# Routing weights spread by DMA from device memory instead of by a matmul, in a fused attention and expert kernel

## The reference, cut to what matters

```
x = x + xattn(layernorm(x), ctx)    # 16 heads of 8: causal self attention plus attention to 64 context rows
h = layernorm(x)                    # 1024 tokens
aff = sigmoid(h @ Wr + br)          # 32 experts
top_v, top_i = top_k(aff, 8);  top_w = top_v / (sum(top_v) + 1e-9)
w_full[t, e] = top_w where e is among token t's eight, else 0
shared = (silu(h @ Wg_s + bg_s) * (h @ Wu_s + bu_s)) @ Wd_s + bd_s
routed = sum over e of w_full[:, e] * ((silu(h @ Wg[e] + bg[e]) * (h @ Wu[e] + bu[e])) @ Wd[e] + bd[e])
x = x + shared + routed
```

## Time and profile before

| | |
|---|---|
| median of 3 runs | 205.09 us (204.45 to 206.31) |
| the profiled execution | 207.16 us |
| its span | 205.40 us, 3982 instructions |
| granted TensorE clock, mean | 0.981 of full speed |
| PE, DVE, ACT, POOL busy | 190.5, 160.7, 135.7, 97.9 us |
| DMA | 10.40 MB, 51 GB/s on average |

### The profile page before, as it was taken

One profiled execution on the slowest core, in us unless ns is written; L12 is line 12 of the kernel. 1 busy time (PEld: TensorE's weight loads), 2 busy tenths in 40 slices (PEclk: granted clock), 3 DMA queues, 4 the chain that ended last, 5 costly groups with the idle time before them and its releaser, 6 DMA issues.

```text
span 205.4 us, 3982 instructions
## 1 busy us (share of the span) xinstructions
PE 190.5 (93%) x1237; PEld 140.4 (68%) x1249; DVE 160.7 (78%) x375; ACT 135.7 (66%) x272; POOL 97.9 (48%) x154
## 2 busy tenths in 40 slices
PE   7969899999999999788999899699899999999993
PEld 2537667777777777666675776488688887887662
DVE  2888997788689977996594889748957879877982
ACT  3544898787898889886779453645545655555571
POOL 6899972343463757339455386665522231100020
PEclk9996999999999999999999999979999999999998
DMA  4365333233342334201201112210000000000003
GB/s 114 94 137 145 100 78 84 50 73 83 71 121 67 77 86 102 54 0 42 65 15 38 38 40 54 51 32 0 3 0 3 0 0 2 0 0 3 0 0 102
DMA packets 20434, 10.40 MB, mean 51 GB/s; under 512 B 11881, under 2 KB 18542, under 8 KB 20414
## 3 DMA queue, kind: packets, MB, share of 16 engines
q1 hardware_dynamic: 19290, 9.24, 18.2%
q0 software_dynamic: 672, 0.69, 1.5%
q10 hardware_dynamic: 452, 0.23, 0.5%
HBM read 4.51 MB, written 0.52 MB: 25 GB/s over the span
## 4 chain that ended last, share of the span: by engine, by line
PE 69%; DVE 11%; issue 8%; ACT 5%; POOL 4%; DMA 1%; DVEq 0%; POOLq 0%; ACTq 0%
PE psum L1358 10%; PE psum L1360 9%; PE psum L1359 9%; PE psum L1461 6%; PE psum L1517 5%; PE psum L1542 4%; PE psum L1554 4%; POOL hid_lo L707 3%; PE psum L1522 3%; PE psum L1564 3%; PE psum L1460 2%; PE psum L1689 2%; PE psum L1526 2%; PE psum L1503 2%; PE psum L1483 2%
## 5 line engine op out<-in xcount | busy, mean ns | idle before, releaser
L925 ACT ACTIVATE gate<-psum,bias_cols 128x512 f32<-128x512 f32 (+2 forms) x35 | 23.5, 675 | 31.5 <-PE psum L1360 31.5
L802 ACT ACTIVATE probs<-psum 128x512 f32<-128x512 f32 x64 | 36.3, 596 | 1.9 <-PE psum L1522 0.8
L707 POOL TENSOR_TENSOR hid_lo<-hid,hid_hi 128x512 fp32r<-128x512 f32 x13 | 16.7, 1287 | 32.7 <-ACT hid_hi L934 30.5
L1302 DVE SCALAR_TENSOR_TENSOR gated<-psum,bias_cols,gate 128x512 f32<-128x512 f32 x32 | 24.0, 749 | 10.5 <-ACT gate L925 7.9
L934 ACT CAST hid_hi<-hid 128x512 fp32r<-128x512 f32 (+1 forms) x33 | 20.2, 613 | 6.3 <-DVE hid L1314 4.5
L1461 PE MATMUL psum<-key_blocks,query_rows 96*128 96x512 f32 x48 | 24.1, 544 | 0.0
L1314 DVE TENSOR_TENSOR hid<-gated,psum 128x512 f32<-128x512 f32 x32 | 21.9, 683 | 2.8 <-PE psum L1689 1.1
L638 POOL TENSOR_TENSOR w_late_lo<-w_ffn,w_late_hi 128x384 fp32r<-128x384 f32 x11 | 12.3, 1116 | 20.0 <-ACT w_late_hi L814 20.0
L663 POOL TENSOR_SCALAR_AFFINE_SELECT probs<-probs 128x512 f32<-128x512 f32 x16 | 10.1, 634 | 20.7 <-ACT probs L802 20.6
L1092 DVE TENSOR_REDUCE row_max<-psum 128x4 fp32r<-128x1024 f32 x16 | 19.4, 1214 | 0.0
L1088 DVE TENSOR_REDUCE row_max<-psum 128x4 fp32r<-128x512 f32 x16 | 11.0, 689 | 8.6 <-PE psum L1461 8.5
(11 more groups left out here) (198 smaller groups left out, 515.1 us busy)
## 6 DMA issues: line engine op xcount, KB each, us to landing
query_rows<-queries SPq DMA_DIRECT2D x46, 64.0 KB, 2.0
key_rows<-keys SPq DMA_DIRECT2D x39, 32.0 KB, 1.9
w_ffn<-in_L_ffn_Wg SPq DMA_DIRECT2D x16, 64.0 KB, 2.0
w_ffn<-in_L_ffn_Wu SPq DMA_DIRECT2D x16, 64.0 KB, 2.1
w_ffn<-in_L_ffn_Wd SPq DMA_DIRECT2D x16, 64.0 KB, 2.1
ckey_rows<-ckeys POOLq DMA_DIRECT2D x12, 32.0 KB, 2.0
key_rows<-keys POOLq DMA_DIRECT2D x9, 32.0 KB, 2.0
x_sb<-in_x SPq DMA_DIRECT2D x2, 128.0 KB, 2.9
```

What stands on the lines that cost most here:

```text
L707: pool.tensor_tensor(hid_lo[:, n % 3, :], hid[:, n % 3, :], hid_hi[:, n % 3, :].bitcast(F32), ALU.subtract).then_inc(pool_lo_done, 1)
L802: act.activation(probs[:, i % 2, c, :], bank(B_ST + c % 2), ACT.Exp, scale=SCALE).then_inc(exp_done, 1)
L925: act.activation(gate[rows_of(n), n % 3, part], psum[of, B_GATE + n % 2, part], ACT.Silu, bias=bias_cols[of, BIAS_GATE + u:BIAS_GATE + u + ...
L1302: dve.scalar_tensor_tensor(out=gated[:, n % 3, :], in0=bank(B_UP + n % 2), scalar=bias_cols[:, BIAS_UP + u:BIAS_UP + u + 1], in1=gate[:, n ...
```

## The change

The spreading matmul goes, with its 0/1 matrix. ACT copies the turned weights a second time, from partitions 64 to 95 of the PSUM bank into `route_rows` (DVE now writes a third, unrounded copy of the weights into `route`, and the row of ones moves from 64 to 96). SP stores them to a tensor in device memory, once per chunk, waits for that store, and then issues one DMA per routed item: it reads the two rows of the unit's experts 64 times each into one of four slots of `wide`. The last six units' weight loads stand between these in SP's queue. DVE multiplies the gate by `wide` first, then takes (up + bias) times that.

```diff
+B_GATES = (0, 1, 4)
+B_UP, B_SIDE = 2, 5
+        route_dram = nc.dram_tensor("route_dram", (EXPERTS, TOKENS), F32, kind="Internal").ap()
 sync:
-            for u in range(SLOTS // 2, UNITS):
+            for u in range(SLOTS // 2, SLOTS + 5):
                 load_unit(sp, u)
+            for n, (u, c) in enumerate(WORK):
+                if n == 1:
+                    load_unit(sp, SLOTS + 5)
+                if LEAD // 2 <= n < LEAD // 2 + UNITS - LEAD:
+                    load_unit(sp, LEAD // 2 + n)
+                if u == SHARED:
+                    continue
+                r = routed(n)
+                cols = slice(c * CHUNK, (c + 1) * CHUNK)
+                if u == 0:
+                    sp.wait_ge(route_rows_ready, 2 * c + 2)
+                    sp.dma_start(route_dram[:, cols], route_rows[RAW:ONES, cols]).then_inc(route_stored, 16)
+                    sp.wait_ge(route_stored, 16 * (c + 1))
+                if r >= WIDE_SLOTS:
+                    sp.wait_ge(gated_done, r - WIDE_SLOTS + 1)
+                sp.dma_start(wide[:, r % WIDE_SLOTS, :],
+                             route_dram[2 * u:2 * u + 2, cols].unsqueeze(1)
+                             .to_broadcast([2, INNER, CHUNK])).then_inc(in_wide_route[r % WIDE_SLOTS], 16)
 scalar:
+                    act.copy(route_rows[RAW:ONES, tokens(b)], psum[RAW:ONES, B_MISC, 0:SEQ]).then_inc(route_rows_ready, 1)
                     act.copy(routeT[:, tokens(b)], bank(B_MISC, SEQ)).then_inc(routeT_ready, 1)
...
-                        act.activation(gate[rows_of(n), n % 3, part], psum[of, B_GATE + n % 2, part], ACT.Silu,
+                        to = gate[INNER:P, n % 3, part] if u == SHARED else gate_bank(n)
+                        act.activation(to, gate_bank(n)[of, part], ACT.Silu,
 vector:
-                    dve.wait_ge(m_up, routed(n + 1))
                     dve.wait_ge(gate_done, n + 1)
-                    dve.scalar_tensor_tensor(out=gated[:, n % 3, :], in0=bank(B_UP + n % 2), ...
+                    dve.wait_ge(in_wide_route[routed(n) % WIDE_SLOTS], 16 * (routed(n) // WIDE_SLOTS + 1))
+                    dve.tensor_tensor(gated[:, n % 3, :], gate_bank(n), wide[:, routed(n) % WIDE_SLOTS, :],
+                                      ALU.mult).then_inc(gated_done, 1)
...
+                    dve.wait_ge(m_up, routed(n + 1))
                     dve.wait_ge(gated_done, routed(n + 1))
-                    dve.tensor_tensor(hid[:, n % 3, :], gated[:, n % 3, :], bank(B_WIDE + n % 2),
+                    dve.scalar_tensor_tensor(out=hid[:, n % 3, :], in0=bank(B_UP + n % 2), ...
 gpsimd:
+            def expand(i):
+                pool.wait_ge(*keys_of(*divmod(i, GROUPS)))
+                pool.wait_ge(m_st, 4 * (i - RING) + 4)
+                for j in (0, 1):
+                    blocks, rows, mine = key_block(i, j)
+                    pool.tensor_tensor(blocks, rows, mine.to_broadcast([ROWS, SEQ]),
+                                       ALU.mult).then_inc(pool_blocks_set, 1)
             for i in range(STEPS):
+                if POOL_BLOCKS <= i + 3 < STEPS:
+                    expand(i + 3)
...
-        POOL_LO = [*range(LEAD), LAST_ITEM - 2]
+        POOL_LO = [*range(LAST_ITEM - 1)]
 tensor:
-            run_idle(8, B_CK)
+            run_idle(12, B_CK)
...
             turn_max(0)
+            run_idle(3, B_MISC)
...
-                        if n >= 2:
-                            pe.wait_ge(gated_done, routed(n - 1))
+                        if n >= 2:
+                            pe.wait_ge(hid_done, n - 1)
...
-                    if u != SHARED and n != LEAD:
-                        spread_routes(n)
```

More of the change, by code:

```diff
@@ L31 @@
 RING = 4
+POOL_BLOCKS = 5
 EXPERTS, TOP, INNER = 32, 8, 64
-SPREADS = 4
-SPREAD_UNITS = 4
+WIDE_SLOTS = 4
+RAW = 2 * EXPERTS
+ONES = 3 * EXPERTS
 PAIRS = EXPERTS // 2
@@ L191, in build @@
         in_ffn = [sem(f"in_ffn{k}") for k in range(SLOTS)]
+        route_stored = sem("route_stored")
+        in_wide_route = [sem(f"in_wide_route{k}") for k in range(WIDE_SLOTS)]
         placed_k = [[sem(f"placed_k{k}_{g}") for g in range(GROUPS)] for k in range(2)]
@@ L402, in lo_done, with gate_bank, affinity_of @@
             return hid_lo_done, VECTOR_LO.index(n) + 1
+        def gate_bank(n):
+            return bank(B_GATES[n % len(B_GATES)])
+        side = bank(B_SIDE, 6 * EXPERTS).rearrange("p (n t e) -> p n t e", n=3, t=2)
+        side_sigmoid, side_affinity, side_logits = side[:, 0, :, :], side[:, 1, :, :], side[:, 2, :, :]
+        def affinity_of(b):
+            return affinity[:, :, :] if b < 2 else side_affinity
         def routed(n):
@@ L717, in _ @@
                     split_unit(ROUND_AT[n + 1])
-            for u in range(LEAD, UNITS):
-                split_unit(u)
-            lower_half(POOL_LO[-1])
         @block.scalar
@@ L891, in left_over @@
                     if name == "router":
+                        act.wait_ge(logits_ready, b + 1)
+                        act.activation(logits[:, :, :], logits[:, :, :], ACT.Identity,
+                                       bias=tiny[:, 0:1]).then_inc(logits_guarded, 1)
                         act.wait_ge(logits_guarded, b - 1)
-                        act.activation(exp_neg[:, :, :], logits[:, :, :], ACT.Silu).then_inc(silu_ready, 1)
+                        act.activation(side_sigmoid, logits[:, :, :], ACT.Silu).then_inc(silu_ready, 1)
+                    elif name == "norm":
+                        act.wait_ge(have_rstd, len(NORM_GROUPS) + b + 1)
+                        for t in range(2):
+                            k = 2 * b + t
+                            act.activation(x2_norm[:, t, :], x1[:, k, :], ACT.Identity, scale=rstd[:, k:k + 1],
+                                           bias=neg_mean[:, k:k + 1]).then_inc(x2_normed, 1)
                     else:
```

139 lines of the change are left out of this document (57 added, 82 removed).

## The result

The changed kernel takes 301.07 us in the median of 4 runs (300.71 to 301.27), the kernel before 204.98 beside it: a ratio of 1.463, with a 95% interval from 1.456 to 1.470. Forecast were 310 us, between 197 and 335. The profiled execution took 301.27 us, its span 299.5.

What follows compares the result with a forecast made beforehand. PE bounds the late expert stage; two engines per spread would make DMA the limit. Copy at 106.3, store 1.9, 32 spreads at 5.8, weights 4.7, landing 2, tail 9.3: span 309.8, say 310 us, range 197 to 335.

Steps and rivals of the forecast that it cites:

- Two engines: Spread DMAs: source of two outer rows is cut in two, 5.8 us per item; 310 us in all, chance 0.55.
- Weights copied at 106.3: Start of the sum: the copy ends at 109.3, less the 3 us gained before.
- 185.6 + 4.7 + 2 = 192.3: Spread stage: 32 spreads at 5.8 us, last six units' weights on the same engines, last landing's fixed part.
- The tail: From gated of item 32 to the end, 9.3 us, taken from the profile of the kernel before.
- Rival A: All sixteen engines carry a spread: span 199.7, 199.4 us by the median, faster than before; chance 0.33.
- round trips at items 0 and 12: Expert stage: waits for copied weights, store and first spread make item 0 2.7 us later and lose 3 us at 12.
- key blocks on POOL: Stretch from 80 to 108: 22 operations at 0.62 us fit POOL's waits; gain 2 us, between 0 and 2.5.
- idle matmuls: Start, 10 to 20 us: they may lift the granted clock from 0.83; gain 1 us, between -1 and +1.7.
- the -2 for swapped operations: Silu bank, PSUM affinity, ACT's copies: may free PE idle time from 107.88 to 149.75; 2 us, 0 to 3.9.
- 32 spreading matmuls: Expert stage: each removed matmul saves PE 0.232 us, 7.4 us in all, the most its steady part can win.
- POOL's lower halves: Expert stage: POOL takes them from DVE, some tenths late where it also splits weights; cost 1 us, 0 to 6.
- Rival C: As sixteen engines, but stores or landings at 5 us and no idle time won back: 209 us, chance 0.04.

Runs made afterwards that it cites:

- two-DMA kernel: The changed kernel with each item's spread as two DMAs, one per expert row copied to 64 partitions, instead of one: 211.61 us, ratio 1.024 against the kernel before.
- without round trips: The kernel with two DMAs per item, but spreads read rows of input x, so nothing is stored and no spread waits for weights: 204.45 us, ratio 0.988.
- the kernel with key blocks alone: The kernel before, with POOL expanding the key blocks of steps 5 to 15, without the seven more idle matmuls; spreading matmul kept: 203.71 us, ratio 0.991.
- the one without round trips and with the normalization back: Two DMAs per item reading x, nothing stored, with sequence 3's second normalization moved from ACT back to DVE; POOL makes only rstd: 200.53 us, ratio 0.969.

## Why the prediction was right, and where its sum was off

**Two engines: shown.** The step that carried the forecast, a cut along the source's outermost rows read from 66 completion packets, is what the packet counts and four kernels show. Of the ways to tell it that the prediction named, the share (0.13 for 0.12), the pitch (5.35 for 5.8 us), the 2 completion packets and `gated` released by the DMA each time (32 of 32) came out. So did POOL's key blocks, 0.62 us each. PE's idle time from 80 to 108 fell to 1.2 us and not to 0.5.

**The terms of the sum.** Weights copied at 106.3: 106.95. Store 1.9: 1.66. From the first spread to the last `gated` 185.6 + 4.7 + 2 = 192.3 was forecast and 288.60 - 108.64 = 180.0 came. This is the mis-sized term: an engine alone moved 131 KB in 5.35 us, 24.5 GB/s, not the 22.6 of the burst; 32 x 0.45 = 14 us. What lies above 32 x 5.35 = 171.2 is 8.8 us, for weight loads and a last landing put at 6.7; 2.2 us of it are the second round trip (7.53 us from item 11 to 12), for which the sum had no term. The estimate of 4.8 us from the Trainium skill's "DMA: Bandwidth & Descriptors", section "Where 436 GB/s comes from", was too low by about as much. The tail took 10.9 us instead of 9.3, with TensorE at 0.50 in it; I had taken the tail of a kernel at full clock. In sum 14 us were too much, all for the rate of an engine, and some 4 us too little: 2.1 behind the spreads, 1.6 in the tail, 0.4 ahead of the first spread. That they offset each other is luck.

**Rival A's number was wrong, though its condition was true in every kernel with sixteen engines.** In spans, the two-DMA kernel took 209.8 where 199.7 was worked out. The runs split this:

| step of the prediction | put at | shown |
|---|---|---|
| round trips at items 0 and 12 | +2.7 +3 | +3.0 and +3.9 of span, +7.2 of time |
| key blocks on POOL | -2 | 0.9%, about -1.8 |
| idle matmuls | -1 | not told apart from 0 |
| normalization of sequence 3 moved to ACT, a part of the -2 for swapped operations | none of its own | +5.7 of span, +3.9 of time |
| 32 spreading matmuls | -7.4 | with the next row together -5.6 of span |
| POOL's lower halves, the other swapped operations | +1, the rest of the -2 | in the row above |

The +3.0 and +3.9 are the distances between the kernels with two DMAs per item and without round trips at item 11 (150.18 against 147.17) and what is added up to item 16 (165.43 against 158.49). The -5.6 is the kernel with key blocks alone against the one without round trips and with the normalization back (span 202.8 and 197.2); by the medians it is 3.2 us, by the ratios 4.7, since the first was profiled in a run above its median and the second in its fastest. For the second reason the 5.7 of span in the table is above the 3.9 of the medians. No run parts the matmuls from the other terms in it. `gated` starts by item, from the timelines of the four kernels:

| `gated` of item | before | key blocks only | no round trip, normalization on DVE | two DMAs |
|---|---|---|---|---|
| 0 | 111.53 | 109.29 | 109.98 | 112.22 |
| 12 | 148.27 | 146.04 | 143.69 | 156.66 |
| 28 | 187.07 | 184.47 | 178.78 | 191.33 |
| end of span | 205.4 | 202.8 | 197.2 | 209.8 |

From key blocks only to no round trip, twelve items save 3.0 us up to item 12 and sixteen 3.3 up to item 28, near 0.232 each. The first of these is in part the clock: from 128 to 136 it is 0.77 to 0.80 in the kernel with key blocks only and 1.00 in the other. From item 16 to 28 an item takes 2.16 us, and not the 2.09 of nine matmuls at 0.232, though PE is busy for all 28 us from 150 to 178; what makes nine matmuls take longer there is open. Behind item 28 nothing is saved: 18.4 us against 18.3. And item 0 is 0.7 us late even without a round trip, since its DMAs stood behind a weight load in SP's queue (issued at 105.97 and 106.52, landed at 109.89).

At item 0 the round trip was sized right: 112.22 - 109.29 = 2.9 us for 2.7. At item 12 `gated` came 6.48 us after that of item 11, against 1.70 before and 2.30 without round trips. Of these 4.2 us 3.9 were still missing at item 16, where 3 were put: the "1.5 items in hand" that I gave PE were not there. The weights of sequence 3 are copied only after `gated` of item 11 (150.18):

```profile
150.94 0.36 ACT L879 COPY route_rows<-psum 32x256 f32<-32x256 f32 x1
...
151.33 0.33 SPq L580 DMA_DIRECT2D route_dram<-route_rows  x1
...
152.98 4.45 SPq L585 DMA_DIRECT2D wide<-route_dram  x7
...
156.66 0.69 DVE L1343 TENSOR_TENSOR gated<-psum,wide 128x512 f32<-128x512 f32 x1 [4.92 <-DMA wide<-route_dram]
```

The step that failed in rival A's sum is "each is swapped for an operation of its size on the same engine or one with idle time". ACT had idle time, 55% busy, but the moved operation brought a wait for POOL with it, and I did not ask, for it, what I asked for every DMA wait: what is queued behind the waiting instruction.

**Rival C's** mechanism, a gain eaten by the round trips, was the nearest to what sixteen engines give: 209 was its number and 209.9 to 211.6 came. That agreement is luck in good part. C had stores or landings of 5 us, and they took 1.65 and 2.7 to 3.2; the moved normalization made up about half of the loss.

## What to carry to other kernels

In these kernels a transfer is cut over the engines along its outermost axis, on the source's side too: before a broadcast read is written, look at which factor stands first, and count completion packets where it matters. The same bytes went from 5.35 us apart to landings of 3.2 us by a swap of two axes, 301 against 210 us.

Idle time on an engine doesn't make it a free place for an operation that waits for another engine; what stands behind that wait in its queue pays. And a result that makes a round trip through device memory costs its store, its issue and its landing, here 3 to 4 us each time, unless other items can go first: with the matmul kept for six items that could not wait, and sixteen engines for the others, the kernel is 3.4% faster than before.

## What the runs showed of the hardware

- Small DVE operations on SBUF can be stretched by POOL as well. In the kernel with key blocks alone two of them took 1.27 and 0.79 us for 2 and 64 elements a row, and each ended just behind a POOL operation; the second, with the affinities in PSUM as the change has them, took 0.23 beside POOL's lower half (timelines of the kernel with key blocks alone, then of the one without round trips):

```profile
121.88 1.29 POOL L726 TENSOR_TENSOR hid_lo<-hid,hid_hi 128x512 fp32r<-128x512 f32 x1 [0.61 <-ACT hid_hi L953]
121.93 1.27 DVE L1224 TENSOR_SCALAR top_sum<-top_sum 128x2 f32<-128x2 f32 x1
...
123.13 1.01 POOL L646 TENSOR_TENSOR w_late_lo<-w_ffn,w_late_hi 128x384 fp32r<-128x384 f32 x1
...
123.43 0.79 DVE L1226 TENSOR_TENSOR affinity<-affinity,r_top 128x64 f32<-128x64 f32 x1
```

```profile
123.57 1.30 POOL L746 TENSOR_TENSOR hid_lo<-hid,hid_hi 128x512 fp32r<-128x512 f32 x1 [0.62 <-ACT hid_hi L979]
...
123.80 0.23 DVE L1249 TENSOR_TENSOR psum<-psum,r_top 128x64 f32<-128x64 f32 x1
```

  From the first to the last operation, sequence 2's weights took 1.4 us instead of 3.1. That part of the change shortens its own operations; no run takes it by itself, so what it is worth in kernel time isn't shown.
- SP can stand in an issue for long when the engines are behind: from 110.95 on, four spread issues in the kernel after took it 12.83 us (0.5, 3.3, 3.6 and 5.2), and none of them stood at a semaphore: the slots were free. With two DMAs per item, two issues took it 1.13 us.
- With sixteen engines 64 reads of one row of 2 KB cost nothing against 8 reads: a 256 KB spread landed in 3.2 us with 64 and in 3.3 with 8. No kernel fills `wide` from rows that are each read once.
